# One image at a time through the scans, the scans' inputs repeated by DMA instead of by matmul, and side steps started image by image

## The reference, cut to what matters

```python
x = x + L0_conv(_gn(x), ...)            # group norm first
t = t + L1_attn(_ln_t(t), ...)
t = t + L1_ffn(_ln_t(t), ...)
# L0_conv, per image:
xc = silu(depthwise3x3(xh) + b)                          # 96 channels, 256 tokens
xs = [rows, columns, rows reversed, columns reversed]    # K = 4 directions
dts, Bs, Cs = split(x_dbl); dts = softplus(dt_w @ dts + b)
h = h * exp(d_t * A) + (d_t * u_t) * B_t                 # 96 channels x 16 states, 256 steps
y = sum over states of h * C_t; add the four directions back in token order; + D * xs
y = layernorm(y) * silu(z) @ out_proj
# L1_attn: q', k' = relu(q @ proj) + eps; context = k'^T v; out = q' context / (q' k_sum)
# L1_ffn: mean-pooled router picks 6 of 12 heads; softmax attention on them; layer norm
```

## Time and profile before

| stretch, us | what runs | PE busy | DVE busy | POOL busy |
|---|---|---|---|---|
| 0 to 41 | group norm, first conv, first step sizes | 20.7 | 29.2 | 14.6 |
| 41 to 313 | the 96 units, from the first scan to the last sum | 228.3 | 245.6 | 180.2 |
| 313 to 461 | the tail | 122.3 | 71.6 | 12.1 |

### The profile page before, as it was taken

The page is one execution under the profiler, slowest core; times in us unless marked ns, Lnnn a source line. Parts: engine busy times, 40 slices in busy tenths (PEclk is TensorE's granted clock), DMA queues, the critical chain, the costliest instruction groups (busy, mean ns, idle before and its releaser), DMA issues. The chain is left out here.

```text
span 461.3 us, 5553 instructions
## 1 busy us (share of the span) xinstructions
PE 371.3 (80%) x1669; PEld 214.3 (46%) x1669; DVE 346.4 (75%) x622; ACT 179.8 (39%) x405; POOL 206.9 (45%) x210
## 2 busy tenths in 40 slices
PE   5825499697887867857999998896989999969691
PEld 4612133142332312323557555553865786958450
DVE  5885989878999999999789898987457356263514
ACT  2565354554563534423243332335225211135340
POOL 7131697867895967774653863451121010000001
PEclk9999889979897987785999999999799989588966
DMA  5502212011121110110101010000000000000000
GB/s 121 106 21 64 56 26 64 23 41 34 23 58 34 47 40 18 40 43 9 47 21 33 11 34 1 0 2 1 2 17 1 1 0 17 2 1 1 1 17 18
DMA packets 15743, 12.69 MB, mean 28 GB/s; under 512 B 7279, under 2 KB 11361, under 8 KB 15713
## 3 DMA queue, kind: packets, MB, share of 16 engines
q1 hardware_dynamic: 15713, 12.33, 11.7%
HBM read 2.62 MB, written 0.79 MB: 7 GB/s over the span
## 5 line engine op out<-in xcount | busy, mean ns | idle before, releaser
L559 POOL TENSOR_TENSOR outp<-state,c_rep 128x512 f32<-128x512 f32 x96 | 126.4, 1321 | 93.0 <-PE y_acc L1397 43.1
L1019 DVE TENSOR_TENSOR_SCAN state<-decay,inp_bc 128x512 f32<-128x512 f32 x96 | 117.2, 1221 | 9.3 <-DVE inp_bc L1010 4.3
L1397 PE MATMUL y_acc<-outp,band 128*96 128x512 f32 x192 | 111.2, 666 | 6.7 <-DVE y_sum L1034 2.6
L732 ACT ACTIVATE decay<-step_bc,a_neg 128x510 f32<-128x510 f32 x96 | 64.9, 683 | 47.0 <-PE step_bc L1384 46.8
L1010 DVE TENSOR_TENSOR inp_bc<-b_rep,inp_bc 128x512 f32<-128x512 f32 x96 | 65.5, 682 | 7.1 <-PE inp_bc L1388 6.9
L1388 PE MATMUL inp_bc<-room_s,spread 96*128 96x512 bf16 x96 | 41.0, 427 | 31.1 <-DVE state L1019 31.0
L494 POOL TENSOR_TENSOR rs<-mv,neg_half 128x2 f32<-128x2 f32 x16 | 11.1, 696 | 120.0 <-DVE mv L1055 119.9
L1384 PE MATMUL step_bc<-room_s,spread 96*128 96x512 bf16 x96 | 39.9, 415 | 12.7 <-DMA room_s<-lo 11.6
L1397 PEld LDWEIGHTS y_acc<-outp,band 128*96 128x96 f32 x192 | 34.3, 182 | 24.7 <-issue 10.3
L1388 PEld LDWEIGHTS inp_bc<-room_s,spread 96*128 96x128 bf16 x96 | 9.9, 103 | 65.9 <-DVE state L1019 56.8
L1384 PEld LDWEIGHTS step_bc<-room_s,spread 96*128 96x128 bf16 x96 | 10.4, 109 | 32.5 <-issue 27.3
(11 more groups left out here) (346 smaller groups left out, 650.8 us busy)
## 6 DMA issues: line engine op xcount, KB each, us to landing
b_rep<-bc SPq DMA_DIRECT2D x64, 32.0 KB, 1.9
c_rep<-bc SPq DMA_DIRECT2D x64, 32.0 KB, 2.0
room_s<-hi SPq DMA_DIRECT2D x24, 64.0 KB, 2.0
room_s<-mid SPq DMA_DIRECT2D x24, 64.0 KB, 2.0
room_s<-lo SPq DMA_DIRECT2D x24, 64.0 KB, 2.0
x_tok<-in_x_dram SPq DMA_DIRECT2D x2, 384.0 KB, 3.8
out_dram<-room_g SPq DMA_DIRECT2D x4, 192.0 KB, 2.0
room_a<-in_L_attn_w_qkv_dram SPq DMA_DIRECT2D x1, 432.0 KB, 6.5
```

The source lines that it names most:

```text
L559: g.tensor_tensor(outp[:, u % SLOTS, :], state[:, u % STATE_SLOTS, :], c_rep[:, n % 2, :], ALU.mult).then_inc(S["outp"], 1)
L732: a.activation(decay[:, u % SLOTS, :, 1:L], step_bc[u % 2][:, :].rearrange("p (b l) -> p b l", b=IMG)[:, :, 1:L], ACT.Exp, scale=a_neg[:, ...
L1019: v.tensor_tensor_scan(state[:, u % STATE_SLOTS, :], decay[:, u % SLOTS, :, :].rearrange("p b l -> p (b l)"), inp_bc[u % 2][:, :], 0.0, AL ...
L1397: t_.matmul(y_acc[0:DI, :], band[:, at:at + DI], outp[:, u % SLOTS, :], start=(g12 == 0), stop=(g12 == UNITS - 1)).then_inc(S["y_mm"], 1)
```

## The change

The diff touches nearly every function. What it does:

- **Layout of the scans.** A unit becomes 16 channels x 8 states (`SN` 8, `GRP` 16) over one image in two *ways* (rows and columns). A scan is one image forwards or backwards: 4 x 2 scans of 12 units (two `PARTS` of 8 states, six `GROUPS` of 16 channels), 96 units as before. The backward ways read `decay`, `drv` and `state` in reversed order instead of having a reversed copy. `y_acc` gathers the 24 units of an image; `add_y` runs once per image.
- **Repeating.** `spread_out`, `hi`/`mid`/`lo` and `stack` go. The steps of a scan are written to DRAM (`keep_step`, 384 KB) and each unit's 16 rows are read back 8 times over (`repeat_step`, 512 KB to `in_rep`, 4 slots). C goes the same way (`keep_c`, `repeat_c`, 256 KB a part). B is made by PE from `xs` with a repeated weight `w_b` (`fill_b`, 16 times) and stays in PSUM.
- **One `drv` bank** takes the product with B, so `drive_of(u)` waits for `scan(u - 1)`. `decay` has 2 slots per direction instead of 3.
- **Front.** Only image 0 is convolved by DVE; images 1 to 3 by PE beside units 0 to 21.
- **Side steps.** Image n may begin at unit 24 (n + 1) + 4. 34 steps each of images 0 and 1 and 9 of image 2 lie beside units (108 steps beside units in all, fronts and weights among them); 55 are left for the tail, in which image 3 runs 11 steps behind image 2. DVE takes a step in PE's own unit; PE takes it ahead of `sum_states(u - 3)`; most steps follow after 1 unit instead of 2. The head steps are `s0 t0 s1 t1 w`: both halves of the weighing (`w0`, `w1`) are one step at the end, and there is one `prob` buffer instead of one per image.
- The ring has 4 banks beside units, 8 in the tail.

```diff
-RING = 3
+RING = 4
-UNITS_AFTER = {step: 1 for step in ("q0", "q1", "q2", "kv00", "kv01", "kv10", "wqk", "wv", "fq", "fk")}
-UNITS_AFTER_ELSE = 2
+UNITS_AFTER = {step: 2 for step in ("yT", "yn", "o", "p", "s0", "s1", "fo")}
+UNITS_AFTER_ELSE = 1
...
-    done, ready = [0, 0], [DIRS * UNITS + FIRST_STEP, DIRS * UNITS + FIRST_STEP + 1]
+    ready = [PER_IMAGE * UNITS * (n + 1) + FIRST_STEP for n in range(IMAGES)]
...
+            def keep_step(n):
+                sp.wait_ge(S["step"], n + 1)
                 if n >= 2:
+                    sp.wait_ge(S["decay"], UNITS * (n - 1))
+                sp.dma_start(step_rows[n % 2], step2[0:DI, :, :].rearrange("p a t -> p (a t)")).then_inc(S["step_kept"], 16)
+            def repeat_step(u):
...
+                if u >= IN_SLOTS:
+                    sp.wait_ge(S["decay"], u - IN_SLOTS + 1)
+                    sp.wait_ge(S["drive"], u - IN_SLOTS + 1)
+                rows = step_rows[n % 2, GRP * g:GRP * (g + 1), :]
+                sp.dma_start(in_rep[:, u % IN_SLOTS, :, :].rearrange("p a t -> p (a t)"),
+                             rows.unsqueeze(1).to_broadcast([GRP, SN, 2 * TOK])).then_inc(S["in_there"][u % IN_SLOTS], 16)
...
             def expo(u):
-                a.activation(decay[:, u % SLOTS, :, 1:L],
-                             step_bc[u % 2][:, :].rearrange("p (b l) -> p b l", b=IMG)[:, :, 1:L],
-                             ACT.Exp, scale=a_neg[:, at:at + 1]).then_inc(S["decay"], 1)
+                for e in range(WAYS):
+                    at = (part * DIRS + WAYS * back + e) * GROUPS + c16
+                    ins = a.activation(decay[:, back, u % DECAY_SLOTS, e, kept],
+                                       in_rep[:, slot, 0, :].rearrange("p (e l) -> p e l", e=WAYS)[:, e, kept],
+                                       ACT.Exp, scale=a_neg[:, at:at + 1])
...
             def drive_of(u):
-                dve.wait_ge(S["bc_inp"], u + 1)
-                v.tensor_tensor(inp_bc[u % 2][:, :], b_rep[:, n % 2, :], inp_bc[u % 2][:, :],
-                                ALU.mult).then_inc(S["drive"], 1)
+                dve.wait_ge(S["in_there"][slot], 16 * (u // IN_SLOTS + 1))
+                if u:
+                    dve.wait_ge(S["state"], u)
+                v.tensor_tensor(drv[:, :], in_rep[:, slot, 1, :], b_bc[part][:, :], ALU.mult).then_inc(S["drive"], 1)
...
             for u in range(SLOT_COUNT):
-                if u + 1 < SLOT_COUNT:
-                    spread_out(u + 1)
-                if u >= Y_LAG:
-                    sum_states(u - Y_LAG)
-                if preparing(u, PRE_RAW):
-                    pre(preparing(u, PRE_RAW))
-                for item in beside[u]:
-                    side(*item)
+                if u % (PER_IMAGE * UNITS) == Y_LAG:
+                    sum_states(u - Y_LAG)
+                for item in beside[u]:
+                    side(*item)
+                if u >= Y_LAG and u % (PER_IMAGE * UNITS) != Y_LAG:
+                    sum_states(u - Y_LAG)
+                for part in range(PARTS):
+                    n = (u - FILL_B[part]) // UNITS
+                    if (u - FILL_B[part]) % UNITS == 0 and 0 < n < SCANS:
+                        fill_b(n, part)
+                if preparing(u, PRE_RAW):
+                    pre(preparing(u, PRE_RAW))
```

More of the change, by code:

```diff
@@ L120, in side_work @@
             ready[n] = u + UNITS_AFTER.get(step, UNITS_AFTER_ELSE)
-    at = {step: i for i, step in enumerate(steps)}
-    done += [0, 0]
     rest = []
@@ new lines, in _ @@
+            keep_c(0)
+            keep_step(0)
+            for u in range(2):
+                repeat_step(u)
+            for i in range(PARTS):
+                repeat_c(0, i)
+            for u in range(2, IN_SLOTS):
+                repeat_step(u)
+            for u in range(SLOT_COUNT):
+                n, at = u // UNITS + 1, u % UNITS
+                later = SECOND_LATER if n == 1 else 0
+                if n < SCANS and at == AT_ROWS + later:
+                    keep_c(n)
+                if n < SCANS and at == AT_STEP + later:
+                    keep_step(n)
+                if n < SCANS and at == AT_REPEAT[0]:
+                    repeat_c(n, 0)
+                if n > 1 and at == AT_REPEAT[1] - UNITS:
+                    repeat_c(n - 1, 1)
+                if u + IN_SLOTS < SLOT_COUNT:
+                    repeat_step(u + IN_SLOTS)
@@ new lines, in pad, with front @@
+            def pad(n):
+                act.wait_ge(S["const"], 8)
+                evac(f"xh_{n}", (xpad[:, n, 1:SIDE + 1, 1:SIDE + 1],
+                                 bank(f"xh_{n}")[0:DI, 0:L].rearrange("p (y x) -> p y x", y=SIDE)))
+            def front(step, n):
+                if step == "z":
+                    src = bank(f"z_{n}")[:, 0:2 * DI].rearrange("p (t c) -> p t c", t=2)
+                    fetched(act, f"z_{n}")
+                    a.copy(z[:, n, :, :], src).then_inc(S["z_kept"], 1)
+                    if n:
+                        act.wait_ge(S["gate_s"], n)
+                    a.activation(ze[:], src, ACT.Exp, scale=-1.0).then_inc(freed(f"z_{n}"), 1)
+                    taken(act, f"z_{n}")
@@ L676, in weights @@
+            for n in range(1, IMAGES):
+                group_normed(n)
+            for n in range(1, IMAGES):
+                pad(n)
             def weights(step):
@@ new lines, in collected, with group_deviations @@
+            def collected(first, last, count):
+                dve.wait_ge(S["gn_stats"], count)
+                for s in range(2 * first, 2 * last):
+                    v.bn_aggr(gmv[:, s, :], gst[:, s, :]).then_inc(S["gn_agg"], 1)
+            def group_deviations(i, cols):
+                w = cols.stop - cols.start
+                fetched(dve, f"gm{i}")
+                dve.wait_ge(S["gn_agg"], cols.stop)
+                v.tensor_copy(gmean[:, cols], bank(f"gm{i}")[0:CK, 0:w]).then_inc(freed(f"gm{i}"), 1)
+                taken(dve, f"gm{i}")
+                v.tensor_tensor(gdv[:, cols], gmv[:, cols, 0], gmean[:, cols], ALU.subtract).then_inc(S["gn_dev"], 1)
+                dve.wait_ge(S["gn_dev"], 2 * i + 1)
+                v.tensor_tensor(gsq[:, cols], gdv[:, cols], gdv[:, cols], ALU.mult).then_inc(S["gn_dev"], 1)
+                dve.wait_ge(S["gn_dev"], 2 * i + 2)
+                v.tensor_tensor(gva[:, cols], gsq[:, cols], gmv[:, cols, 1], ALU.add).then_inc(S["gn_var"], 1)
@@ L913, in _ @@
+            group_bias(0, one)
+            turned_stats(2, 1)
+            for c in range(2):
+                turned_stats(3, c)
+            collected(1, IMAGES, 2 * IMAGES)
             for e in range(2):
@@ L1290, in _ @@
             done(ins)
-            group_means(0)
+            turn_input(2)
+            group_vars(0, one)
+            turn_input(3)
             b_ = begin("w_xp")
@@ L1300, in _ @@
             done(ins)
[L1301 removed]
+            taken(pe, "w_in")
+            inner(0)
+            group_means(1, others)
+            group_vars(1, others)
             b_ = begin("w_alog")
[L1303 removed]
+            pe.wait_ge(S["w_alog"], 32)
             done(t_.transpose(b_[:, 0:DIRS * UNITS], alog[:], ident[0:DIRS * UNITS, 0:DIRS * UNITS]))
[L1305 to L1312 removed]
             b_ = begin("w_fold")
@@ new lines, in pre, with fill_b @@
+            def pre(n):
+                b_ = begin(f"d{n}")
+                for e in range(WAYS):
+                    ins = way(b_, n, e)
+                done(ins)
+            def fill_b(n, part):
+                if n:
+                    pe.wait_ge(S["drive"], UNITS * (n - 1) + GROUPS * (part + 1))
+                i = n // PER_IMAGE
+                pe.wait_ge(S["xs"], i + 1)
+                for e in range(WAYS):
+                    k = WAYS * (n % PER_IMAGE) + e
+                    ins = t_.matmul(b_bc[part][:, e * L:(e + 1) * L], w_b[:, k, part, :], xs[:, i, e, :], start=True, stop=True)
+                ins.then_inc(S["b_there"], 1)
@@ L1595, in side @@
                     done(ins)
-            front("z", 0)
+            for n in range(1, IMAGES):
+                inner(n)
             b_ = begin("d0")
```

805 lines of the change are left out of this document (340 added, 465 removed).

## The result

The changed kernel takes 506.02 us (502.57 to 507.29, 4 runs) against 461.56 us of the kernel before in the same comparison: a ratio of 1.0951, 95% interval 1.0885 to 1.1017. It is 9.5% slower; forecast were 456 us, in a range of 441 to 475. The profiled execution took 507.3 us, of which 505.5 are the span.

The account below looks back on a forecast made before the run. The kernel was taken as bound by DVE beside the units, then by PE in the tail. Profiled: 463.0 + 1.5 (start) + 28 (units) - 34.8 (tail) = 457.7 us; median 456, range 441 to 475.

Parts of the forecast that it names:

- Start: Before and around the first scan: first scan at 43.4 us, about 1 us regained in the next units, +1.5 us net.
- costed at nothing: In the start: DVE's and PE's new waits before the first step sizes add nothing, `pre_inp(0)` ending at 34.35 us.
- DVE work in the units: Beside the 96 units: side work moved in raises DVE's busy time from 245.6 to 276 us.
- the wait of `drive_of(u)`: Between bare units on DVE: the product's wait for the scan ahead costs 0.11 us in some 55 units, +6 us.
- DMA: Transfers beside the units: about 56 MB at 228 GB/s, 245 of 300 us, hidden behind the units.
- PE in the units: TensorE beside the units: repeats go, fills of B, a conv and products come; under 230 of 300 us.
- DVE idle in the units: DVE's waits beside the units: 24 us of idle time, between 14 and 38.
- two places per image: DVE waits at `at` (about 4 us) and `w` (about 2.5 us), in two images each: +13 us.
- The rival of the same-unit wait: In the units DVE stands at side products PE has not made, PE waiting for ACT: 473 us, chance 0.24.
- Tail: After the units: 66 us of PE work, 18 of waits, 29.5 last chain; 113.5 instead of 148.3, -34.8 us.
- the last chain: Image 3 alone at the end of the tail: 27.8 us plus 1.7 for half of `w`, 29.5 us.
- the short tail of 103 us: Rival for the tail: two chains cover each other as four did, 103 us in all, time 442, chance 0.22.

Follow-up runs that it names:

- a_sums: The changed kernel with TensorE's sum, fill with B and next step sizes' product ahead of the side product: 502.5 us, ratio 1.0818.
- b_all3: The kernel before with side steps on DVE in PE's unit, steps one unit apart and side products ahead of sums: 493.3 us, ratio 1.0674.
- a_clock: The changed kernel with unread identity products on TensorE filling its waits in the tail, and one ring bank fewer there: 495.2 us, ratio 1.0735.
- a_sp: The changed kernel with two units instead of one behind six kinds of step, 63 image steps in the tail instead of 55: 479.8 us, ratio 1.0410.

## Why the prediction was wrong, point by point

The forecast for the profiled execution was 457.7, measured were 507.3 us. With the cut at the last sum, the difference of 49.5 is 2.6 in the start, 27.9 in the units and 19.0 in the tail.

*Start.* Forecast was +1.5 in all: the first scan 2.4 us later, and about 1 given back. It is 4.1 us later. `pre_inp(0)` ends at 36.2 us, not at 34.35: "costed at nothing" was wrong by 1.9 us. The 9.0 us from there to the scan came out (45.1 - 36.2 = 8.9), in part by luck: the write took 3.0 us, from its issue to that of the first read, and not 3.8; the read 4.9, to 44.13, and not 4.4; the rest 1.0.
```profile
36.26 0.31 SPq L455 DMA_DIRECT2D step_rows<-step  x1
39.24 1.25 SPq L467 DMA_DIRECT2D in_rep<-step_rows  x2
```
Nothing was given back: the first four units take 13.3 us (13.4 before), and the first 28 take 1.9 us more.

*DVE work in the units: right.* 276 us were forecast, 279.2 measured. Reversed scans cost nothing. The term for the wait of `drive_of(u)` came out by luck. Two bare units in a row are 2.05 us apart, 0.21 over the earlier trace rows, where 0.11 was forecast; but only 28 times, not 55, does nothing but the product lie between two scans, which makes 5.9 us. And most of the 0.21 is idle and not busy time: 1.22 and 0.70 us of work in 2.05. What makes the 3.2 us of difference no run shows. DVE's busy time is not work alone: with the very same steps beside the units it was 274.8 us in `a_sums`. A second bank for the product, which would free it from the scan ahead, was not tried: it would have to come out of the ring.

*DMA: right.* The transfers hide, at 252 GB/s. A 512 KB read lands after 4.9 us (4.4 forecast), the 384 KB write after 3.8 as forecast, as medians over all of them. The Trainium skill's "DMA: Bandwidth & Descriptors", section "Anatomy of one DMA", whose figures are for transfers issued by GpSimd, would make them 3.2 and 2.9 us, an estimate from the page. The first write, with 3.0 us, agrees with it closely; the reads do not, and the measurement decides. The difference bears on the start alone, and not on the units.

*PE in the units: its clock was not costed.* The forecast had PE under 230 of 300 us. It is busy 256.8 of 329.1 us, at a granted clock of 0.83 instead of 0.90; at full clock that is 213 us, and 206 before. So a sum takes 727 ns on average where the earlier trace rows have 666, and the products that DVE waits for come later. How much of DVE's idle time this makes is open: no run kept the clock up in the units alone. It isn't all of it, since `b_all3` has the same 49.8 us of idle time at 0.87.

*DVE idle in the units: the step that failed.* I wrote that most products "are there in time", that two places per image are not, and took 24 us. The two places were right, with 15.6 us in all. But 49.9 us is the total, above the upper bound of 38 too: beside the two places, for which 13 was taken, 11 us were forecast and 34 measured. The error is in costing waits of DVE alone, place by place, against PE's time for one product. With steps one unit apart PE itself stands: 25.4 us at the turns behind the two normalizations, and it stands ahead of its sums, so that POOL waits 122.5 us for them, and ahead of the product for the step sizes, so that DVE and ACT wait for those as well (`spl`, 5.7 us, 3.5 in the kernel before; the 11 us between 175.74 and 186.75). The runs show it from three sides: spacing six kinds of step takes 12 us of idle time off, 9.6 of them at `at` and `w`; two units nearly everywhere with the sums first bring it to 28.9; and the new rules in the old layout bring it up from 27 to 49.8 with one step moved in. The rival of the same-unit wait had the right sign and nearly the right mechanism ("PE itself waits for ACT"), at a price of 473. Its other half, that the missing lag of DVE is to blame, holds only in the kernel before (+26 us); in the changed kernel the lag made it slower at one unit's distance and made no difference at two. Why the two layouts differ in this is not settled.

*Tail: the term that was mis-sized.* Forecast were 66 us of PE work, 18 of waits and 29.5 for the last chain; measured are 84.7, 16.6 and 30.0. The waits and the last chain were right, and the short tail of 103 us did not come. The 66 us came from a stretch at a granted clock of 0.89: at full clock that is 59 us, and 84.7 at 0.70 is 59 too. So the work was right and its clock was not. `cx` took 5.30 us where the earlier trace rows have 2.87, `at` 5.34 and 5.30 instead of 2.77:
```profile
383.00 5.30 PE L1486 MATMUL ring<-v,room_a 128*128 128x34 f32 x24 [1.07 <-ACT v L780]
388.11 0.64 PE L1457 MATMUL b_bc<-ident,room_f 128*96 128x128 f32 x2
388.90 5.34 PE L1496 MATMUL b_bc<-cbd,room_b 128*128 128x34 f32 x24
...
429.55 5.30 PE L1496 MATMUL ring<-cbd,room_b 128*128 128x34 f32 x24 [0.81 <-issue]
```
The stretch in which the tail begins ran wholly at the lower of the two levels, with PE busy for 23.2 of 25.8 us, behind waits of 2.0 us ahead of the last sum and 1.2 us behind it:
```profile
374.20:400.00 25.80, 23.23 (x77) 17.80 (x78) 6.59 (x23) 1.91 (x6) 1.98 (x3) 0.50 0.00 0
```
That the lower clock of the tail cost 24 us of busy time, and that filling the waits raises it, is shown by `a_clock`. That PE has more waits since fewer chains cover each other is the likely reason, but not shown apart from it.

*What lay under both.* The forecast assumed that a step moved out of the tail takes its PE time with it, about 1 us a step (34.8 us for 36 steps). The tails measured are 147 us with 91 steps (before), 141 and 144 with 69, 131 with 66, 129 with 63, and 131 (`a_sums`: 140) with 55. Below some 66 steps nothing seems to be gained, but these tails have different clocks: 0.78 with 66 steps, 0.75 with 63, and 0.67 (0.62) with 55. With the waits filled, 55 steps take 120.9 us and 63 take 127.8 and 129.4, which is about 1 us a step again. So the steps did take their time with them, and the lower clock of what was left ate it. Whether image 3's chain of 33 links, which can't begin before the last sum, sets a length further down no run shows. Meanwhile a step moved in costs DVE, which is the bound there: between `a_sp` and the changed kernel, eight steps and their order make 12.5 us of its busy time.

## What to carry to other kernels

When several engines, each in order, pass a dependent chain of small steps along beside a main loop, the distance between links has to hold the slowest link on *every* engine, with what stands ahead of it in each queue; a link that is late on one engine can stop the main loop on all. Work that is moved from a tail into a loop whose bound engine has to do it is paid for there, and the tail need not shrink with it: here 55 steps took as long as 63, at a lower clock. When a TensorE-bound stretch is thinned out, its remaining work must not be costed at the clock of the full stretch.

## What the runs showed of the hardware that was not expected

- In the changed kernel's tail, with PE busy 100.4 of 131.3 us, the granted clock was 0.67; with the waits filled it was 0.85, and the same matmuls took 76.3 us. In the kernel before, 121.7 us at 0.84 became 98.5 at 0.98.
- A scan over a row in reversed order costs what a forward one does: 1219 to 1222 ns over all 96.
- Where a DVE product waits for the scan ahead of it, it starts 1.32 us after that scan's start instead of 1.14, and the scan 0.73 us after it: 2.05 us for a unit instead of 1.84.
- The transfers of the first 28 units, mostly the reads of 512 KB into `in_rep`, ran at 227 GB/s with the DMA engines 89% busy over 80 us, and DVE waited only 1.8 us for them in all the units.
